# A three-branch graph layer on one core: the attention's chain of steps spread over more slots, and edge and row preparation reordered

## The reference

```
xn = layernorm(x)
# 1. graph attention over the edges (src, dst)
Wh = xn @ W + b
e  = leaky(Wh@a_dst [dst] + Wh@a_src [src] + a_b)
att = softmax of e over the edges of one src
gnn = relu(segment_sum(att * Wh[dst], src))
# 2. linear attention and a feed-forward block
q, k, v = xn@Wq+bq, xn@Wk+bk, xn@Wv+bv          # 8 heads of 32
q_phi, k_phi = phi(q), phi(k)                   # phi(x) = x+1 if x>0 else exp(x)
kv, k_sum = sum_l k_phi v, sum_l k_phi
out = (q_phi kv) / (q_phi k_sum + 1e-6)
m = layernorm(xn + out@Wo + bo)*g1 + b1
mix = layernorm(m + relu(m@W1+b1)@W2 + b2)*g2 + b2
x = x + gnn + mix
# 3. top-2 of 6 experts, three dense layers each, on layernorm(x)
x = x + combined experts
```

## Time and profile before

| | us |
|---|---|
| median of 3 runs | 2283.14 (2281.95 to 2285.73) |
| profiled execution | 2283.29, span 2281.3 |
| TensorE busy | 1872.5 (82%) |
| VectorE busy | 1666.6 (73%) |
| ScalarE busy | 1441.3 (63%) |
| GpSimd busy | 1196.2 (52%) |
| mean granted TensorE clock | 0.909 of full |

### The profile page before, as it was taken

How to read it: one execution, slowest core, us unless ns; L and a number is a source line. 1 busy time by engine, 2 the same in 40 slices (tenths; PEclk the granted TensorE clock), 3 DMA queues, 4 the chain that set the end, 5 groups by cost and what they waited for, 6 DMA issues and landing times. The chain is left out here.

```text
span 2281.3 us, 49594 instructions
## 1 busy us (share of the span) xinstructions
PE 1872.5 (82%) x10102; PEld 1507.4 (66%) x10102; DVE 1666.6 (73%) x5291; ACT 1441.3 (63%) x4425; POOL 1196.2 (52%) x1169
## 2 busy tenths in 40 slices
PE   1588858599963899999999999999998572799996
PEld 0344436377752777877878778788787462688885
DVE  7687878887663888888888888898897642355543
ACT  3566639334320888989889889898897650233332
POOL 2000000036565777777777777777772277255554
PEclk9799988788765999999999999999999565799998
DMA  4312101121102444444443444444441543255553
GB/s 144 88 50 58 56 28 47 30 75 48 39 25 67 118 122 116 118 123 118 121 117 110 123 114 116 122 119 120 116 116 41 187 161 136 58 91 96 93 96 53
DMA packets 133863, 215.45 MB, mean 94 GB/s; under 512 B 42781, under 2 KB 89052, under 8 KB 133572
## 3 DMA queue, kind: packets, MB, share of 16 engines
q0 software_dynamic: 61920, 132.16, 23.9%
q1 hardware_dynamic: 66990, 72.68, 10.7%
q10 hardware_dynamic: 4662, 7.46, 1.1%
HBM read 150.28 MB, written 56.51 MB: 91 GB/s over the span
## 5 line engine op out<-in xcount | busy, mean ns | idle before, releaser
L1375 POOL DMA_INDIRECT area<-wh_table,area x788 | 768.5, 975 | 260.3 <-issue 251.8
L1702 PE MATMUL bank<-area 128*126 x1960 | 483.2, 389 | 31.0 <-ACT area L1622 15.0
L1702 PEld LDWEIGHTS bank<-area 128*126 128x126 f32 x1960 | 348.9, 188 | 104.6 <-issue 56.2
L1408 DVE TENSOR_SCALAR area<-iota_row,area 128x126 f32<-128x126 f32 x980 | 353.5, 369 | 21.1 <-ACT area L1575 17.2
L1608 ACT ACTIVATE area<-iota_row,area 128x126 f32<-128x126 f32 x735 | 285.8, 389 | 0.0
L2193 POOL DMA_INDIRECT out_dram<-area x108 | 169.0, 1565 | 166.0 <-DVE area L2254 149.2
L1622 ACT ACTIVATE area<-area 128x126 f32<-128x126 f32 x735 | 237.0, 386 | 0.4
L572 POOL DMA_INDIRECT sorted_slots<-area x112 | 137.1, 1224 | 116.6 <-DVE area L930 84.7
L1561 ACT ACTIVATE area<-bank 125x512 bf16<-125x512 f32 x245 | 145.3, 593 | 78.6 <-DVE area L1422 75.8
L1722 PE MATMUL bank<-area 128*128 128x250 f32 x800 | 188.4, 378 | 6.6 <-ACT area L1629 3.5
L565 POOL IOTA acc_mem<- 128x788 f32 x1 | 0.8, 792 | 365.5 <-DVE area L839 365.5
(11 more groups left out here) (417 smaller groups left out, 4050.3 us busy)
## 6 DMA issues: line engine op xcount, KB each, us to landing
area<-moe_rows SPq DMA_DIRECT2D x54, 264.0 KB, 2.7
area<-wh_table,area POOLq DMA_INDIRECT x788
area<-area SPq DMA_DIRECT2D x17, 388.5 KB
wh_table<-area SPq DMA_DIRECT2D x50, 126.5 KB
xn<-in_x_dram SPq DMA_DIRECT2D x25, 250.0 KB
xt_rows<-area SPq DMA_DIRECT2D x50, 125.0 KB, 2.3
area<-xt_rows SPq DMA_DIRECT2D x25, 250.0 KB
x_rows<-area SPq DMA_DIRECT2D x25, 250.0 KB
```

What stands on the lines that cost most here:

```text
L1375: g.indirect_dma_start(out=gath[:, (i + GT) % RS, :], out_offset=None, in_=table, in_offset=bass.IndirectOffsetOnAxis(ap=idx_tab[:, i:i + ...
L1408: ins = V.tensor_scalar(xm[:, b, t, :], iota_row[:, :], rowl[:, j % 10, t:t + 1], fetched(j, D)[:, t:t + 1], ALU.is_equal, ALU.mult)
L1702: last = T.matmul(bank[US[b]][0:RW, 0:WROW], sm[:, b, t, :], gath[:, bass.ds(place + t, 1), 0:WROW].rearrange("p a w -> p (a w)"), start=( ...
```

## The change

It has two parts.

**Edges and first statistics.** The edge arrays are loaded in smaller parts, and the tail is filled in place before its load, so that each preparing step is one instruction over 128 rows. Only the source part is prepared ahead of the masks; the destination part becomes `destinations`, behind the scans. `weights` and the statistics of the first ten tiles move ahead of the first scan. Projection steps start with slot 0 instead of slot 2. Statistics of later groups move two slots later, and the row statistics of tiles 10 to 19 run five to a slot in slots 7 and 8. SyncE issues nine of the 25 chunks of `x` ahead, the others one by one between stores, and the twelve later weights at tile 16. GpSimd's fill of the slot tables waits until the edges have landed.

**The attention's chain.** Offsets of the steps change:

| step | engine | before | after |
|---|---|---|---|
| `inverses` | TensorE | 10 | 11 |
| `divide` | VectorE | 11 | 12 |
| `o` | TensorE | 12 | 13 |
| `attend_sum` | VectorE | 13 | 15 |
| `root` | ScalarE | 14 | 16 |
| `attend_norm` | VectorE | 15 | 18 |
| `normal` | ScalarE | 16 | 19 |

```diff
-FIRST, STEPS, SG = 2, NT + 4, 10
+STEPS, SG, X_FIRST = NT + 4, 10, 9
...
         def group_at(b):
-            return (b - 1) // 5 if b % 5 == 1 and b < 5 * (NT // SG) else None
+            return (b - 3) // 5 if b % 5 == 3 and SG // 2 < b < 5 * (NT // SG) else None
         def steps_at(b):
-            first = max(0, (b - FIRST) * STEPS // (NT - FIRST))
-            return range(first, max(first, (b + 1 - FIRST) * STEPS // (NT - FIRST)))
+            return range(b * STEPS // NT, (b + 1) * STEPS // NT)
...
-                for i in range(NC):
-                    sp.dma_start(xn[...], x[...]) ...
-                for to, frm in loads_late:
-                    sp.dma_start(to, frm, ...).then_inc(w_late, 16)
+                for i in range(X_FIRST):
+                    load_x(i)
                 for t in range(2):
                     keep_turned(t)
+                    load_x(X_FIRST + 2 * t)
+                    load_x(X_FIRST + 2 * t + 1)
                 for t in range(NT):
                     if t + 2 < NT:
                         keep_turned(t + 2)
+                    if X_FIRST + 4 + t < NC:
+                        load_x(X_FIRST + 4 + t)
+                    if t == NC - X_FIRST:
+                        for to, frm in loads_late:
+                            sp.dma_start(to, frm, ...).then_inc(w_late, 16)
                     sp.wait_ge(p_row, t + 1)
...
+                g.wait_ge(edges_in, 128)
                 for i in range(2):
                     g.dma_start(slots[i] ...
...
+                step(V.tensor_copy(srcf, srci))
+                V.memset(wpos, 0.0)
                 step(V.tensor_scalar(cumi, srcf, 0.5, 1.0 / R, ALU.add, ALU.mult))
+                V.memset(E_[:, 0, :], 0.0)
                 step(V.tensor_copy(q0, cumi))
+                V.memset(G_[:, 0:1], 0.0)
                 step(V.scalar_tensor_tensor(cmp, q0, float(R), srcf, ALU.mult, ALU.is_gt))
                 step(V.tensor_tensor(blk, q0, cmp, ALU.subtract))
                 step(V.scalar_tensor_tensor(srcf, blk, -float(R), srcf, ALU.mult, ALU.add))
+                V.tensor_scalar(v1h, srcf, 1.0, 8.0, ALU.add, ALU.mult).then_inc(edges_ready, 1)
+                def destinations():
+                    step(V.tensor_scalar(dst_bits, dsti, 10, None, ALU.logical_shift_right))
+                    step(V.tensor_copy(v0h, dst_bits))
+                    step(V.tensor_tensor(v1h, v1h, v0h, ALU.add))
+                    step(V.tensor_scalar(dst_bits, dsti, 1023, None, ALU.bitwise_and))
+                    step(V.tensor_copy(v0h, dst_bits))
+                    step(V.memset(bpos, -1.0e6))
...
+                weights()
+                for t in range(SG):
+                    moments(t)
+                statistics(0)
+                less_mean(0)
                 scan(0)
...
                 dve.wait_ge(placed, NT)
+                destinations()
...
# VectorE's attend
-                    c = chunk_at(slot, 15)     # attend_norm, then 13 attend_sum, 11 divide
+                    c = chunk_at(slot, 18)     # attend_norm, then 15 attend_sum, 12 divide
# ScalarE's attend
-                    c = chunk_at(slot, 16)     # normal, then 14 root
+                    c = chunk_at(slot, 19)     # normal, then 16 root
# TensorE's attend
-                    c = chunk_at(slot, 12)     # o, then 10 inverses
+                    c = chunk_at(slot, 13)     # o, then 11 inverses
```

More of the change, by code:

```diff
@@ L310, in gps_kernel @@
         cums = [take(COLS) for _ in range(2)]
-        v0h, v1h, hih, loh = (take(COLS // 2).bitcast(F16) for _ in range(4))
+        v0h, v1h = (take(COLS // 2).bitcast(F16) for _ in range(2))
+        hilo = take(COLS)
+        hih, loh = (hilo[:, i * COLS // 2:(i + 1) * COLS // 2].bitcast(F16) for i in range(2))
+        dst_bits = hilo.bitcast(I32)
         iotaH = take(HI * WI // 2).bitcast(F16).rearrange("p (h i) -> p h i", i=WI)
@@ L611, in proj @@
                         keys(s - 3)
-                dve.wait_ge(edges_in, 96)
+                last = E - (L - 1) * COLS
+                V.memset(srci[96:128, last:COLS], N)
+                V.memset(dsti[96:128, last:COLS], 0).then_inc(edges_ready, 1)
+                dve.wait_ge(edges_in, 128)
                 dve.wait_ge(consts, 1)
-                last = E - (L - 1) * COLS
-                V.memset(srcf, float(N))
-                step(V.memset(dhi, 0))
-                V.tensor_copy(srcf[0:96, :], srci[0:96, :])
@@ L619, in _ @@
-                V.tensor_copy(srcf[96:128, 0:last], srci[96:128, 0:last])
-                step(V.tensor_copy(srcf[96:127, last:COLS], srci[96:127, last:COLS]))
-                V.tensor_scalar(dhi[0:96, :], dsti[0:96, :], 10, None, ALU.logical_shift_right)
-                V.tensor_scalar(dhi[96:128, 0:last], dsti[96:128, 0:last], 10, None, ALU.logical_shift_right)
-                V.tensor_scalar(dhi[96:127, last:COLS], dsti[96:127, last:COLS], 10, None, ALU.logical_shift_right)
+                step(V.tensor_copy(srcf, srci))
@@ L630, in _ @@
-                V.tensor_scalar(dlo[96:128, 0:last], dsti[96:128, 0:last], 1023, None, ALU.bitwise_and)
-                V.tensor_scalar(dlo[96:127, last:COLS], dsti[96:127, last:COLS], 1023, None, ALU.bitwise_and)
                 step(V.scalar_tensor_tensor(srcf, blk, -float(R), srcf, ALU.mult, ALU.add))
-                step(V.tensor_copy(cmp, dhi))
-                step(V.tensor_scalar(srcf, srcf, 1.0, 8.0, ALU.add, ALU.mult))
-                V.tensor_tensor(v1h, srcf, cmp, ALU.add)
-                V.memset(wpos, 0.0)
@@ L637, in _ @@
[L637 to L641 removed]
+                V.tensor_scalar(v1h, srcf, 1.0, 8.0, ALU.add, ALU.mult).then_inc(edges_ready, 1)
+                dve.wait_ge(edges_ready, 2)
+                def destinations():
[5 more added lines that the diff above has]
+                    step(V.memset(bpos, -1.0e6))
@@ L705, in _ @@
                     i = group_at(b)
-                    for t in range(0, SG) if b == 1 else range(SG + 2 * (b - 2), min(NT, SG + 2 * (b - 1))) if b > 1 else ():
+                    for t in range(SG + 5 * (b - 7), SG + 5 * (b - 6)) if 7 <= b <= 8 else range(2 * SG + 2 * (b - 9), min(NT, 2 * SG + 2 * (b - 8))) if b > 8 else ():
                         moments(t)
@@ L709, in _ @@
                         statistics(i)
-                    if i == 0:
-                        weights()
                     if b + 1 < NT:
@@ L781, in attend @@
                 def attend(slot):
+                    c = chunk_at(slot, 18)
+                    if c is not None:
+                        attend_norm(c)
                     c = chunk_at(slot, 15)
                     if c is not None:
-                        attend_norm(c)
-                    c = chunk_at(slot, 13)
-                    if c is not None:
                         attend_sum(c, at(c) % 2)
-                    c = chunk_at(slot, 11)
+                    c = chunk_at(slot, 12)
                     if c is not None:
@@ L971, in _ @@
                 act.wait_ge(consts, 1)
[L972 removed]
+                act.wait_ge(edges_ready, 2)
                 def mask(b, first, slot, freed):
@@ L1079, in attend @@
                 def attend(slot):
-                    c = chunk_at(slot, 16)
+                    c = chunk_at(slot, 19)
                     if c is not None:
                         normal(c, at(c) % 2)
-                    c = chunk_at(slot, 14)
+                    c = chunk_at(slot, 16)
                     if c is not None:
@@ L1227, in attend @@
                 def attend(slot):
-                    c = chunk_at(slot, 12)
+                    c = chunk_at(slot, 13)
                     if c is not None:
                         o(c)
-                    c = chunk_at(slot, 10)
+                    c = chunk_at(slot, 11)
                     if c is not None:
```

38 lines of the change are left out of this document (18 added, 20 removed).

## The result

| kernel | median | runs | lowest to highest | profiled span | granted clock |
|---|---|---|---|---|---|
| before | 2282.55 us | 4 | 2281.68 to 2285.73 | 2281.3 | 0.909 |
| after | 2340.87 us | 4 | 2330.86 to 2345.35 | 2338.8 | 0.893 |

The changed kernel takes 1.0247 of the time before, with a 95% interval of 1.0212 to 1.0281: 2.5% slower, or 58 us. The forecast was 2329 us, +46, in a range of 2280 to 2366.

The account below looks back on a forecast made before the run. It took a transfer wait to stall the scans, VectorE to be busy 71.8 of 83 us in placing, and TensorE to bound the table loop. From 2283.3 us: -28 + 26 + 1 + 47 = +46, so 2329 us, range 2280 to 2366.

Parts of the forecast that it names:

- the placing loop: Placing loop: VectorE waits for the next chunk's denominators, period 14.0 us as taken, +26 us.
- the table loop: Table loop: o waits for divide twice a cycle, cycle 30.4 us as taken, +47 us.
- The scans: Scans: stall gone and earlier start, less added costs; tile 49's product at 270 against 298.1, -28 us.
- the stall: Scans: ScalarE's wait for the first store of a transposed tile goes, gaining 18.6 us.
- the start: Scans: the first product comes near 34.5 us, 12.6 us earlier than 47.09.
- Rival (d): Scans: chunks land later or stores stall again, -13 in place of -28, 2344 us; chance 14%.
- the working: Both loops: step times added at full clock; placing period 11.7 us, table cycle 26.3 us (old order 21.7).
- the long gap: Table loop: TensorE's gap of about 4 us, lowering the clock at 70% of up to 3.9 us.
- the short one: Table loop: TensorE's gap of about 2.5 us, lowering the clock at 35% of up to 3.9 us.
- rival (b): Both loops: all at the half clock, placing +36 and table +77, 2372 us; chance 9%.
- (a): Both loops: gaps do not lower the clock, placing +11 and table +14, 2280 us; chance 13%.
- (c): Both loops: spreading works, TensorE never waits, cycle 21.7 and placing period 9.7, 2230 us; chance 6%.

Follow-up runs that it names:

- old_queue: Changed kernel with the seven old attention offsets and SyncE's old order (all 25 chunks of x, late weights, then stores), early start kept: 2277.54 us, 0.9999 of before.
- fill: Changed kernel plus four matmuls of no use, 256 columns each, ahead of TensorE's wait for divide: 2290.57 us, 1.0066 of before.
- front_fill: Changed kernel with the seven old attention offsets, plus two unused matmuls ahead of o, in the table loop for every other chunk: 2227.58 us, 0.9779 of before.
- attend_first: Changed kernel with the attention steps of a table step's first slot ahead of its one-hot on VectorE: 2313.15 us, 1.0143 of before.
- sum_back: Changed kernel with attend_sum, root, attend_norm and normal back at 13, 14, 15 and 16: 2299.59 us, 1.0097 of before.
- o_back: Changed kernel with inverses, divide and o back at 10, 11 and 12: 2274.75 us, 0.9974 of before.

## Why the prediction was right, and where its sizes were off

The waits were where the forecast put them, but that its sum came so near (+46 for +57.5) is in part luck: the placing loop was forecast 9 us too high and the table loop 21 too low.

**The scans: right in sum (-26.6 for -28), with two terms that are not independent.** The chunk landed at 24.57 for an estimated 23.6, the first product came at 34.21 for 34.5, tile 49 at 271.51 for 270, and no wait for `xt_rows` is left on ScalarE. But I wrote 18.6 us for the stall and 12.6 for the start as if each could be had alone. `old_queue` shows that the 12.6 can't: the start alone gives nothing, as the store is issued only when all that stands ahead of it has been. Whether the 18.6 can be had alone is not shown. Rival (d), the start gives little, is out for this kernel; `old_queue` shows what it would have looked like.

**`destinations`: right.** Hidden in VectorE's idle time ahead of the block sums, with 5.71 us of it left.

**The placing loop: the mechanism right, the size too large (+17.2 for +26).** The wait for L1218 is there in seven of the periods, at 1.5 to 4.0 us, and `divide` stands at the end of what waits behind it. The first of the six periods ran at the full clock, from the `o` at 320.11 to the one at 331.74. VectorE's timeline and TensorE's:

```profile
324.72 0.17 DVE L769 TENSOR_SCALAR area<-bank 125x16 f32<-125x16 f32 x1 [2.07 <-PE bank L1218]
```

```profile
331.74 1.58 PE L1236 MATMUL bank<-area 128*125 128x256 f32 x3 [3.88 <-DVE area L776]
```

That is 11.63 us, with a wait of 2.07, for the 11.7 and 2 of the working. All six, between the `o` at 320.11 and at 399.56, are 79.45 / 6 = 13.24 us, where I took 14.0 between 11.7 at the full clock and 15.6 at the half. On TensorE's timeline of the kernel before, the same six periods lie between these two:

```profile
346.39 1.10 PE L1222 MATMUL bank<-area 128*125 128x256 f32 x4 [0.86 <-DVE area L765]
...
407.94 1.13 PE L1222 MATMUL bank<-area 128*125 128x256 f32 x4 [1.22 <-DVE area L765]
```

That is 61.55 / 6 = 10.26 us each and not the 9.96 that I took, since one of them holds the slow stretch of the earlier trace rows. Six times the difference is 17.9, the measured term within 0.7 us. Mis-sized were the share of half clock, 60% taken where (13.24 - 11.7) / 3.9 is 40%, and the base by 0.3 us.

**The table loop: the mechanism right, the size too small (+67.6 for +47).** Both waits of `o` for `divide` are there. I had 26.3 us a cycle at the full clock and 34.1 with both gaps at their full price, and took 30.4 by giving the long gap 70% and the short one 35%. The step that failed is the choice of these two shares. TensorE's clock fell with both waits in every cycle; of the seven cycles five took 33.8 to 34.0 us and two 31.7 to 31.9, in the mean 33.3. That is nearly the full price of both, so the term came near the +77 of rival (b). One cycle, from VectorE's one-hots:

```profile
564.62 1.95 DVE L926 TENSOR_TENSOR area<-acc_mem 128x3444 f16<-128x3444 f16 x1 [2.39 <-PE bank L1263]
...
576.78 1.95 DVE L926 TENSOR_TENSOR area<-acc_mem 128x3444 f16<-128x3444 f16 x1 [6.99 <-PE bank L1263]
...
582.67 1.95 DVE L926 TENSOR_TENSOR area<-acc_mem 128x3444 f16<-128x3444 f16 x1
...
598.67 1.95 DVE L926 TENSOR_TENSOR area<-acc_mem 128x3444 f16<-128x3444 f16 x1 [2.44 <-PE bank L1263]
```

The second, third and first step take 12.2, 5.9 and 16.0 us, for a working of 9.6, 6.3 and 10.4 at the full clock. So the price is full in the sum and not gap by gap: the short gap cost 2.6 us, and the long one 5.6, more than the 3.9 taken for a full price, since `q` ran at half speed too. In `fill` the same steps take 9.6, 5.9 and 11.8, the last with 1.5 us of added matmuls in it, so the 26.3 was sound.

The rows held a hint at the shares. The kernel before measured 24.57 us a cycle where the same working gave 21.7, and `front_fill` confirms the 21.7 at the full clock (21.8). So one gap of 1.47 us had already cost 2.9 us in the mean, over 70% of 3.9, and the forecast gave 35% to a longer one. In that kernel's table loop the clock fell with five of the seven such gaps; TensorE's timeline behind the one at 564.89:

```profile
566.20 1.90 PE L1222 MATMUL bank<-area 128*125 128x256 f32 x4
```

The prediction's sentence on what the rule of the page "TensorE: Matmul & The Clock Gate" of the Trainium skill (its section on psum-queue depth-cycling) alone would give, all gaps costing, was nearly right here (+67.6 for +77) and far off for the placing loop (+17 for +36). In the placing loop the clock fell with each of the six gaps of 3.9 to 4.2 us as well, but for 3.4 us with the first two and 6.8 with the others, where the table loop had up to 13.7, and in the later periods it fell while TensorE was still waiting. For the `o` at 358.17, whose gap began at 354.3, the windows view of TensorE alone:

```profile
355.80:362.50 6.70, 4.33 (x9) 0.50 0.05 13
```

Of these 6.7 us at half speed TensorE was idle for 2.4, and that part cost nothing.

**The long gap.** I had it as one wait of about 4 us. It is 1.41 for VectorE's overlong third step, a burst of 0.6 us, and 1.82 for `divide`. With three short gaps a cycle, none over 2.3 us, the clock was 0.72.

**The rivals.** (a), the clock holds, would have needed what `fill` had to buy with added matmuls; even then the kernel is 0.7% slower than before, where the rival had it 0.1% faster. (b), all at the half clock, is nearly what the table loop did (+67.6 for its +77) and not what the placing loop did (+17 for its +36); its 2372 is 31 too high. (c), the spread works, fell by the order rows: `attend_first` shows what the one-hot ahead of the attention steps costs.

**What stays open.** The placing loop took 97.5, 103.7 and 104.0 us in three kernels that have the same order of instructions in it, and 80.3, 83.1 and 78.9 in the three with the old order. The clock goes with it (0.78, 0.71, 0.73 and 0.86, 0.79, 0.86), and the work before it starts at other moments. Which moment decides was not tried, and these are one profile each. For that reason what `sum_back`, `o_back` and `attend_first` say of single steps is good to some 6 us only.

## What to carry to other kernels

Where two engines hand work to each other in a fixed cycle, an offset of a step is not slack: put the consumer's instructions of one cycle side by side, and see that what releases the other engine stands ahead of what waits for it, and ahead of the long instruction of its own slot. When TensorE has short recurring gaps, work out the cycle once at the full clock and once with what stands behind every gap at the half, and try matmuls of no use in the gap before anything else: it is a small edit, and it tells the clock's share from the order's, if it is made to the old order too. Two gains that end at the same transfer may be one gain; ask of each whether it is left when the other is undone.

## What the runs showed of the hardware

- In the changed kernel's table loop TensorE's granted clock fell to 0.50 behind a gap of 2.29 us, and, where gaps of 1.41 and 1.82 us stood close together, during the second, in cycle after cycle. In the kernel before it fell with five of the seven gaps of 1.45 to 1.47 us in the table loop. In `front_fill`, with gaps of 0.45 and 0.54, it stayed at 1.00 from 448 to 600 us.
- Matmuls that do nothing, put where TensorE waits, shortened the cycle: 5.6 us of them in a cycle of two chunks (1.96 and 3.65) took 6.0 us off the cycle in `fill`, and 1.10 us a cycle took 2.6 off in `front_fill`.
- A load of `x` with 125 partitions keeps few of the DMA engines busy. In the kernel before, the windows view at the time of these loads:

```profile
40.00:60.00 20.00, 10.21 (x29) 5.08 (x29) 17.51 (x30) 8.39 (x15) 0.00 (x0) 0.95 0.34 120
```

A share of 0.34 of 16 engines is 5.4 of them, at 120 GB/s. At that rate 25 chunks of 250 KB take some 52 us by estimate, near the 57 us for which SyncE issues them. The page "DMA: Bandwidth & Descriptors" of the Trainium skill says, in its section "Why a DMA increments its semaphore by 16 and not by 1", that a copy runs on the largest number of engines up to 16 that divides its slowest dimension, which is 5 for 125 rows; the share agrees with it. Whether loads cut otherwise would shorten the stall was not tried.
